# A path through DRAM replaced by direct copies, and a root moved in ScalarE's order, in a four-layer kernel

## The reference

```python
def _ref(x, ...):                       # triangle layer, three times
    xn = _ln(x, norm_scale, norm_bias)
    left = (xn @ Wl + bl) * mask * sigmoid(xn @ Wlg + blg)
    right = (xn @ Wr + br) * mask * sigmoid(xn @ Wrg + brg)
    out_gate = sigmoid(xn @ Wog + bog)
    out = _banded_ingoing(left, right, 4)          # 9 diagonals of left times shifted rows of right
    out = _ln(out, out_norm_scale, out_norm_bias) * out_gate
    return out @ Wo + bo

def _mamba(xs, ...):                    # scan layer over the 256 rows of x, for each column
    ...
    h = dA * h + dt * B * x             # one step of the recurrence
    ...

x = x + _L0_conv_ref(_gn(x), ...)       # then L1, L2
x = x + _L3_conv_ref(_gn(x), ...)
```

## Time and profile before

| | us |
|---|---|
| median of 3 runs | 2884.79 |
| lowest and highest | 2880.19, 2886.39 |
| the profiled execution's own time | 2880.51 |
| its span, first to last instruction | 2878.7 |

### The profile page before, as it was taken

The page is one execution under the profiler, slowest core; times in us unless marked ns, Lnnn a source line. Parts: engine busy times, 40 slices in busy tenths (PEclk is TensorE's granted clock), DMA queues, the critical chain, the costliest instruction groups (busy, mean ns, idle before and its releaser), DMA issues.

```text
span 2878.7 us, 37843 instructions
## 1 busy us (share of the span) xinstructions
PE 2323.4 (81%) x13030; PEld 731.3 (25%) x13030; DVE 2331.4 (81%) x2040; ACT 1855.0 (64%) x2533; POOL 2045.4 (71%) x1188
## 2 busy tenths in 40 slices
PE   4889778897789877578887887878888788887887
PEld 1333122441224321122222222222222222222221
DVE  5655566655657455499999999999999999999999
ACT  3624556345563435378777787777877778777773
POOL 2554244552346422289999999999999999999998
PEclk9999999999999999789999999999999999999998
DMA  4797315984249865766767767676676767767774
GB/s 161 249 334 243 104 56 169 361 280 124 67 128 338 289 195 161 160 163 175 191 168 185 177 176 190 168 186 173 178 187 170 185 175 179 187 170 184 174 180 125
DMA packets 262172, 537.26 MB, mean 187 GB/s; under 512 B 43816, under 2 KB 155184, under 8 KB 260576
## 3 DMA queue, kind: packets, MB, share of 16 engines
q1 hardware_dynamic: 231152, 467.91, 58.5%
q0 software_dynamic: 18720, 63.19, 7.4%
q10 hardware_dynamic: 12112, 3.74, 0.7%
HBM read 395.41 MB, written 139.33 MB: 186 GB/s over the span
## 4 chain that ended last, share of the span: by engine, by line
DVE 25%; issue 18%; PE 12%; ACT 11%; DMA 3%; SPq 1%; POOL 1%; ACTq 0%; DVEq 0%; POOLq 0%
DVE m_hs L493 13%; DVE m_pb L488 12%; ACT m_da L426 4%; PE m_pb L290 2%; DMA t_tile<-band_out 2%; PE t_bank L1069 1%; ACT L374 1%; PE m_py L264 1%; ACT L356 1%; ACT m_act L362 1%; PE m_misc L220 1%; PE m_py L255 1%; PE t_bank L1059 1%; DMA late<-right_factor 1%; ACT m_act L368 1%
## 5 line engine op out<-in xcount | busy, mean ns | idle before, releaser
L517 POOL TENSOR_TENSOR m_hs<-m_hs,m_cs 128x1024 f32<-128x1024 f32 x511 | 1197.7, 2357 | 125.4 <-DVE m_hs L493 85.1
L493 DVE TENSOR_TENSOR_SCAN m_hs<-m_da,m_pb 128x1024 f32<-128x1024 f32 x416 | 951.4, 2287 | 14.4
L290 PE MATMUL m_pb<-m_dtx,late 64*128 64x512 f32 x1664 | 503.6, 679 | 230.6 <-DVE m_hs L493 223.2
L488 DVE TENSOR_TENSOR m_pb<-m_pb,m_bs 128x1024 f32<-128x1024 f32 x416 | 502.9, 1209 | 14.2 <-PE m_pb L290 14.2
L426 ACT ACTIVATE m_da<-m_dtb,late 128x1020 f32<-128x1020 f32 x414 | 464.5, 1144 | 3.7 <-DMA m_dtb<-dt_rows 1.5
L1573 POOL TENSOR_TENSOR t_xc<-t_xc,big 128x512 f32<-128x512 f32 x96 | 120.0, 1270 | 313.4 <-DVE big L1437 313.2
L290 PEld LDWEIGHTS m_pb<-m_dtx,late 64*128 64x128 f32 x1664 | 156.1, 201 | 550.3 <-DVE m_hs L493 310.7
L264 PE MATMUL m_py<-m_hs,late 128*32 128x512 f32 x2048 | 277.0, 613 | 2.5 <-POOL m_hs L517 2.5
L1303 ACT ACTIVATE t_sq<-t_bank 128x512 f32<-128x512 f32 x192 | 106.1, 596 | 209.7 <-PE t_bank L1142 209.5
L1570 POOL TENSOR_TENSOR t_sq<-big 128x512 f32<-128x512 f32 x96 | 102.9, 1082 | 182.9 <-ACT big L1285 108.1
L1316 ACT ACTIVATE t_gate<-t_bank,t_small 128x512 f32<-128x512 f32 x192 | 121.4, 683 | 165.1 <-PE t_bank L1069 165.0
(11 more groups left out here) (169 smaller groups left out, 3775.8 us busy)
## 6 DMA issues: line engine op xcount, KB each, us to landing
m_dtb<-dt_rows SPq DMA_DIRECT2D x510, 512.0 KB, 5.5
late<-right_factor POOLq DMA_DIRECT2D x102, 512.0 KB, 6.6
right_factor<-t_tile SPq DMA_DIRECT2D x192, 256.0 KB, 4.1
t_tile<-band_out SPq DMA_DIRECT2D x183, 256.0 KB, 4.0
band_out<-t_vwin SPq DMA_DIRECT2D x48, 512.0 KB
band_out<-t_vwin SPq DMA_DIRECT2D x48, 480.0 KB
dt_rows<-m_dt SPq DMA_DIRECT2D x64, 256.0 KB, 4.6
t_xc<-in_x_cm SPq DMA_DIRECT2D x8, 1024.0 KB, 12.4
```

The lines of the kernel that those rows point to most:

```text
L290: m = nc.tensor.matmul(pb[s % 2][:, half(n)], spread[rows, dg, :], dtx[par][rows, half(q)], start=True, stop=True)
L488: nc.vector.tensor_tensor(products, products, bs[q][:, :], ALU.mult).then_inc(u_done, 1)
L493: nc.vector.tensor_tensor_scan(hs[:, g % H_RING, :], decays, products, 0.0, ALU.mult, ALU.add).then_inc(h_ready, 1)
L517: nc.gpsimd.tensor_tensor(hs[:, g % H_RING, :], hs[:, g % H_RING, :], cs[q][:, :], ALU.mult).then_inc(hc_ready, 1)
```

## The change

1. `store_x`, the DRAM tensor `x3` and the gathers from it are gone. `hand_over` now copies from `xc` straight into `shared.xm`, from SBUF to SBUF, again in pieces of 64 floats. SyncE issues the first half (rows 0 to 127, 16 DMAs of 256 KB) in steps 74 to 77, four in each, behind that step's loads, and the rest at its end with ScalarE, each behind the `x_done` that frees its target. SyncE waits for all of them before the barrier, so the waits in the scan layer go. For this the rows lie differently in the groups of `xc`: `half` no longer alternates with the row pair, and a few offsets follow from that.
2. `root3` stands behind the squares and y1 of its step in ScalarE's order, and in front of the sigmoids of units below `LATE`. It was first in the step.
3. TensorE and VectorE wait at first only for avg and center32 (`first_consts`), and TensorE for the other constants behind `prepare(0)`.
4. The table set for silu is loaded at the end of the triangle layers' block, not behind the barrier.

Left out below: offsets that follow from the rows' new places, the removed waits of VectorE, arguments and declarations.

```diff
@@ -317,9 +317,6 @@
-                a.preload_act_table_set("silu_and_others")
-                a.wait_ge(shared.x_in, shared.X_LOADS)
-                a.wait_ge(shared.x_in_pool, shared.X_LOADS_POOL)
...
@@ -856,12 +850,11 @@
-        x_stored = [sem(f"x_stored{i}") for i in range(4)]
-        names = ("consts", "zeroed", "w_loaded", "stat_done", "gn_rs", "gn_mid", "gn_out",
+        names = ("first_consts", "consts", "zeroed", "w_loaded", "stat_done", "gn_rs", "gn_mid", "gn_out",
...
-        (consts, zeroed, w_loaded, stat_done, gn_rs, gn_mid, gn_out,
+        (first_consts, consts, zeroed, w_loaded, stat_done, gn_rs, gn_mid, gn_out,
...
@@ -884,12 +877,17 @@
-        X_GROUP = lambda n: 0 if n < 16 else 1 if n < 24 else 2 if n < 28 else 3
-
-        def hand_over(eng, lo, hi, groups=range(COLS // HID), arrived=shared.x_in):
-            for g in groups:
-                eng.dma_start(shared.xm[C * g:C * g + C, lo:hi, :], x3[:, lo:hi, HID * g:HID * g + HID]
-                              ).then_inc(arrived, 16)
+        def hand_over(eng, first, last, p, halves=(0, 1)):
+            units = xc[:, BAND + first * UNIT:BAND + last * UNIT].rearrange("c (r k) -> c r k", k=COLS)
+            lo, hi = first_row(first, p), first_row(last - 1, p) + 4
+            for half in halves:
+                g = 2 * p + half
+                for col in range(COLS // HID):
+                    eng.dma_start(shared.xm[C * col:C * col + C, lo + half:hi:2, :],
+                                  units[C * g:C * g + C, :, HID * col:HID * col + HID]).then_inc(shared.x_in, 16)
+
+        def all_done(eng, n):
+            eng.wait_ge(x_done, 2 * UNITS * (LAYERS - 1) + n)
...
@@ -941,13 +939,6 @@
-
-                def store_x(n):
-                    sp.wait_ge(x_done, 2 * UNITS * (LAYERS - 1) + n + 1)
-                    for g in range(4):
-                        row = first_row(n, g // 2) + (g % 2 ^ n % 2)
-                        sp.dma_start(x3[:, row:row + 3:2, :],
-                                     x_unit(n)[C * g:C * g + C, :].rearrange("c (r k) -> c r k", r=2)).then_inc(x_stored[X_GROUP(n)], 16)
...
@@ -969,13 +960,18 @@
-                            for n in st["bc3"]:
-                                store_x(n)
-                sp.wait_ge(x_stored[2], 16 * 4 * 4)
-                hand_over(sp, first_row(24, 0), first_row(28, 0))
-                hand_over(sp, first_row(24, 1), first_row(28, 1))
-                sp.wait_ge(x_stored[3], 16 * 4 * 4)
-                hand_over(sp, first_row(28, 0), first_row(16, 1))
+                            if 0 <= s - A3_STEP[27] < 4:
+                                all_done(sp, UNITS)
+                                hand_over(sp, 0, 16, (s - A3_STEP[27]) // 2, ((s - A3_STEP[27]) % 2,))
+                all_done(sp, 24)
+                hand_over(sp, 16, 24, 0)
+                all_done(sp, 28)
+                hand_over(sp, 24, 28, 0)
+                all_done(sp, 30)
+                hand_over(sp, 24, 28, 1)
+                all_done(sp, 32)
+                hand_over(sp, 28, 32, 0)
+                sp.wait_ge(shared.x_in, shared.X_LOADS)
...
@@ -1065,7 +1061,7 @@
-                        hs = g % 2 ^ n % 2 ^ (flip & p)
+                        hs = g % 2 ^ n % 2 ^ (flip & (p ^ n % 2))
...
@@ -1100,9 +1096,11 @@
 
-                pe.wait_ge(consts, 16 * len(const_loads))
+                pe.wait_ge(first_consts, 32)
                 for l in range(LAYERS):
                     prepare(l)
+                    if l == 0:
+                        pe.wait_ge(consts, 16 * len(const_loads) - 32)
                     for s, st in enumerate(STEPS):
...
@@ -1138,7 +1136,7 @@
-                                    o = HID * (hs ^ p)
+                                    o = HID * (hs ^ p ^ n % 2)
...
@@ -1191,7 +1189,7 @@
-                    a.dma_start(dst[tuple(slice(None) for _ in dst.shape)], w[name]).then_inc(consts, 16)
+                    a.dma_start(dst[tuple(slice(None) for _ in dst.shape)], w[name]).then_inc(consts if i > 1 else first_consts, 16)
...
@@ -1276,8 +1274,6 @@
                             root(l, "root1", b, P)
-                        for b in st["root3"]:
-                            root(l, "root3", b, P)
                         for n in st["a1"]:
...
@@ -1293,8 +1289,8 @@
                         for n in st["a3"]:
-                            tables(SIGS)
                             if n == 0 or n >= LATE:
+                                tables(SIGS)
                                 open_gates(l, n)
...
@@ -1304,8 +1300,11 @@
                                 take_y1(l, n)
+                        for b in st["root3"]:
+                            root(l, "root3", b, P)
                         for n in st["a3"]:
                             if 0 < n < LATE:
+                                tables(SIGS)
                                 open_gates(l, n)
...
@@ -1322,16 +1321,15 @@
-                a.wait_ge(x_stored[1], 16 * 4 * 8)
-                hand_over(a, P, first_row(24, 0))
-                a.wait_ge(x_done, 2 * UNITS * (LAYERS - 1) + 28)
-                hand_over(a, first_row(16, 1), first_row(24, 1))
+                all_done(a, 28)
+                hand_over(a, 16, 24, 1)
+                all_done(a, 32)
+                hand_over(a, 28, 32, 1)
...
-                a.wait_ge(x_stored[3], 16 * 4 * 4)
-                hand_over(a, first_row(28, 1), ROWS)
+                a.preload_act_table_set("silu_and_others")
...
@@ -1571,11 +1569,6 @@
                             nc.gpsimd.tensor_tensor(x_unit(n), x_unit(n), xn_unit(n), ALU.add).then_inc(x_done, 1)
-                            if l == LAYERS - 1 and 18 <= n < 26:
-                                if n == 18:
-                                    g_.wait_ge(x_stored[0], 16 * 4 * UNITS)
-                                half_, g = divmod(n - 18, 4)
-                                hand_over(g_, HID * half_, HID * half_ + HID, (g,), shared.x_in_pool)
                         for t in STEPS[s + 2]["band"] if s + 2 < len(STEPS) else ():
...
@@ -1602,7 +1595,7 @@
-        return np.array([[P * w_ + HID * p + 2 * r + (half ^ r // 2 % 2) for r in range(HALFROWS)] for w_ in range(2)])
+        return np.array([[P * w_ + HID * p + 2 * r + half for r in range(HALFROWS)] for w_ in range(2)])
...
```

26 lines of the change are left out of this document (11 added, 15 removed).

## The result

The kernel after takes 2867.84 us (median of 12 runs, 2860.07 to 2877.09), the kernel before 2885.34 us in the runs beside them (2880.19 to 2896.22). The ratio is 0.9936 with a 95% interval of 0.9923 to 0.995. So it is faster, by 18.5 us (0.64%, from the ratio) where 41.4 were forecast, and its time lies 3.8 us above the range of 2826 to 2864.

What follows compares the result with a forecast made beforehand. VectorE bounds the untouched scan layer, some 1680 us; gains lie in the triangle layers and the seam, about 1200 us. 2.8 + 9.6 - 1.4 + 30.4 = 41.4 us gained gives 2841 us, range 2826 to 2864.

Steps and rivals of the forecast that it cites:

- part 3: Third layer and seam to the scan layer: x copied straight into the scan layer's tile, gain 30.4 us.
- The new wait for the other constants costs nothing: Start: the chain behind the first matmul ends after 30.1, so waiting there for the other constants adds nothing.
- Bounds 0 and 3.2: Step 54: limits in us on the cost of the root behind the squares, put at 1.4 us.
- TensorE takes the variance at 753.1: Step 76, second layer: point in the new order worked out, ahead of the next gate projection to 755.2.
- The 3.5 us of step 76: Second layer: c3 behind the root starts at 756.9 instead of 760.38, 3.5 us earlier.
- the forecast 2.7: Step 70: gain in us from the root behind the squares, between 2.0 and 3.4.
- Rival (c): Reordering gives nothing, as the root's Exp or second table load arrives as late as now: 2852 us, chance 0.09.
- R: Time of the third layer's Ln of step 60, 1047.12 in the kernel before, from which its later times are counted.
- Rival (b): Copies run at SyncE's issue rate, 148 GB/s: gain 19.7 us in all, 2861 us, chance 0.13.
- Rival (d): Copies' reading and writing share a path, about 105 GB/s: slower than before, 2890 us, chance 0.06.
- some 3 us late: Third layer: delay of a tile load behind the copies in SyncE's queue, taken not to bind.
- rival (a): Copies are faster, 273 GB/s needed, and x_done binds: gain 50.8 us in all, 2830 us, chance 0.22.

Runs made afterwards that it cites:

- trial 3.2: Changed kernel with its copies replaced by trials: SyncE alone copies 8.39 MB within SBUF, 256-byte pieces, 64 partitions to the same 64; 70.0 us, 125 GB/s.

## Why the prediction failed

Three steps failed: the rate of the copies, what step 54 costs, and the order of TensorE in the steps of the roots. By ratios to before, and 2885 us (the rows for steps 70 and 76 and for the copies don't cut the third layer in the same way, their sum does):

| step | forecast, us | measured, us | from |
|---|---|---|---|
| constants | -2.8 | -2.6 | 0.9991 |
| step 54, three layers | +4.2 | +11.8 | 0.9936 / 0.9895 |
| steps 70 and 76, three layers | -12.4 in two, the third in part 3 | -6.6 in three | 0.9918 / 0.9895 |
| direct copies | -30.4 | -21 | 0.9918 / 0.9991 |
| sum | -41.4 | -18.5 | 0.9936 |

**Constants: right, with one term too low.** TensorE's first matmul starts at 27.32 (forecast 27.3), and the first Ln of a block root 2.8 us earlier than before. "The new wait for the other constants costs nothing" holds in this trace; in the run of the constants alone TensorE waited 1.10 us there for the last constant, and 0.3 to 1.4 us in the six other kernels with the split constants.

**Step 54: right in its mechanism, wrong in its size.** The wait of TensorE on the bank of the gates is there, and the gap between squares' end and sigmoids is 4.5 us as forecast. But the step lost 2.5 us at full clock where I had 1.4, and I let the cost end with the wait. Across the layers and kernels above, in seven of nine cases the gap was followed by a stretch with a lower granted clock, in none of 21 without the gap. "Bounds 0 and 3.2" was too low: 3.9 was measured. The earlier trace rows showed the step with its cover; the gap itself, and so what follows it, was in no row that I had read.

**Steps 70 and 76: a step was missing, and the row I started from was a slow one.** My order by hand went "TensorE takes the variance at 753.1", 2.2 us behind the c3 of 750.92. That variance is the first of a new block, and the code makes it wait for the Ln of the block before (`first_square`); it started at 759.64, 0.05 us behind the end of the Ln and 4.25 us behind its c3. Before, the variance waited for squares and the Ln had long run, so the wait could not be seen in the earlier trace rows, only in the code. The 3.5 us of step 76 come apart like this: I went from the 9.46 us of the earlier trace rows to 6.0. In that row the granted clock had fallen (mean 0.82 from c3 to c3); at full clock the old order takes 7.9 us and the new one 7.3. So 1.3 us are the missed wait, 1.5 the lower clock that I had taken for a part of the order, and 0.6 are left. In step 70, where the row of before stood at full clock, the forecast 2.7 became 0.6 as well. The rest of the 2.2 us a layer that were measured came from something I had not thought of: the clock fell less often behind the shorter gap. Rival (c) named the place ("rest on an order worked out"), but by another cause, and at 0.09. With the projection in front of the variance the wait for the Ln falls from 2.14 to 1.13 us in every undisturbed case, which shows the cause; of the 10.7 us of that run it is the smaller part.

**Copies: the rate.** I took 213 GB/s from gathers out of DRAM, "since pieces and destination are the same". The source was not: from SBUF the copies run at 145 alone, 152 in the trace, 168 together with tile loads. From the first copy to the landing it took 62 us; I had 51.2, and that from the tile load ahead of it. The first copy was issued at R + 72.4 where I had 68.5 for that load: 2.0 us of it is the gain of step 70 that was missing, the rest the load's own issue. The two are the 14.8 us by which the landing came late (R + 134.5, forecast R + 119.7). Rival (b) had the rate (148) with the wrong reason, the issue rate. Rival (d), sharing of reading and writing, had a part of the reason and too low a rate (105): copies within the same 32 partitions run at 119, the rest at 153. I had set the bounds of the rate at 148 and 273, and gave the lower end 0.13. The only rows with SBUF as the source were the stores of the earlier trace rows (8 of 64 KB in 4.80 us, 109 GB/s by issue), and the sum left them out; that was the ground to move weight down. The tile loads behind the copies were also priced too low: "some 3 us late" became 107.3 us from Ln to Ln in the third layer, forecast "not above 100", and 92.9 with the copies spread out.

For rival (a) I had named the Trainium skill (DMA: Bandwidth & Descriptors, "Why small descriptors are slow (HBM only)"), by which transfers within SBUF don't suffer from small pieces. The runs don't agree: 215 GB/s with 256-byte pieces against 340 with 1 KB over 128 partitions, 145 against 181 over 32. The measurement decides. The other rule of the Trainium skill that I named (SBUF — State Buffer, "Door 1: The DMA port swizzle") fits the side of the forecast that held, DRAM into 32 partitions at 196 under its 218, though one window of the earlier trace rows showed 226; and by it 64 neighbouring partitions reach no more ports than 32, which agrees with trial 3.2: 125 GB/s within 64, 119 within 32.

**What the scan layer did.** From L202 to the end of the span it took 1676.2 us before, 1672.1 after; in the other eight profiles of kernels without trials it took 1671.8 to 1677.4, in those with the path over DRAM and in those with the copies. So the 4.1 us belong to no part of the change that I can show; they make up a part of the 21 us of the copies, of which the stage itself shows 14.4 (L202 at R + 140.9 with the old order, 155.4 before). How much of the rest is the third layer's start and how much the scatter between executions stays open. Part 4 of the change has no run of its own, but the table load is hidden in both kernels: at 1180.57 and ahead of the landing now, at 1198.28 and ahead of the x of the scan layer before.

## What to carry to other kernels

A rate for a transfer has to come from a row with the same source as well as the same target and the same pieces; where none is there, one short trial costs less than the bet. Before work is moved behind something on one engine, list what the other engines write into the memory that it reads: the wait that takes over may not occur once in the old trace. A gap of 2 us or more on TensorE is priced with the slower stretch that may follow, and a row in which the granted clock had already fallen is no baseline: look at the same place in the other layers first. Reordering the waiting engine's own queue (here one projection in front of one variance) may be worth more than the move that made the gap.

## What the runs showed of the hardware

- Copies from SBUF to SBUF in 256-byte pieces between groups of 32 partitions: 144 to 146 GB/s over all pairs of groups, from one, two or three queues. Within it, from one queue: 119 where both groups are the same, 153 where they differ. GpSimd's queue alone is slower (125).
- Two queues that read from groups 64 partitions apart reach 180, and 198 if they write to such groups too; at 128 partitions one queue reaches 215, and with 1 KB pieces 340.
- ScalarE's 24 issues of copies into full queues took 18.3 us of its time; what stands behind them waits as long.
- TensorE's granted clock behind a gap in its matmuls, at the places of the table above: in steps 71 and 77 it fell in 12 of 17 cases after gaps of 2.7 to 2.8 us, in 2 of 16 after 2.1 us and in none of 22 after 1.1; in step 55 in 4 of 6 after 2.2 us and in 3 of 3 after 3.2. Where it was 0.57 over the 8 us behind the gap, eight matmuls that take 1.09 us at full clock took 1.98.
